# Transformer block on one core: the batch loop written out, maxima computed in head pairs, losses by gram matrices

## What is computed

```
x = layernorm(x + self_attention(x))       # three rounds over the first 16 tokens of a batch; the other rows get its bias alone
q, k, v = heads(x @ Wq), heads(ctx @ Wk), heads(ctx @ Wv)     # 16 heads of 16, ctx has 1601 rows
x = layernorm(x + softmax(q k' / 4 + mask) v @ Wo)
base = x @ W_base + b_base
h[n] = relu(x @ W_enc[n] + b_enc[n])                          # 8 experts, 64 wide
losses[n] = mean((h[n] @ W_dec[n] + b_dec[n] - x) ** 2)       # per batch
a = connected_idx[argmin(losses)]
x = layernorm(x + base + relu(x @ W_down[a] + b_down[a]) @ W_up[a] + b_up[a])
```

## Time and profile before

| | |
|---|---|
| median of 3 runs | 2031.69 us (2022.25 to 2032.2) |
| span of the profiled execution | 2026.6 us |
| own time of the profiled execution | not given beside its span |
| first stage, up to the first score of batch 0 | 0 to 234.0 us |
| batch 0 | 234.0 to 420.0 us |
| a full batch (the fourth) | 857.8 to 1078.1 us |
| last batch | 1735.3 to 1952.8 us |
| tail of the last batch | 1952.8 to 2026.6 us |

### The profile page before, as it was taken

One profiled execution on the slowest core, in us unless ns is written; L12 is line 12 of the kernel. 1 busy time (PEld: TensorE's weight loads), 2 busy tenths in 40 slices (PEclk: granted clock), 3 DMA queues, 4 the chain that ended last, 5 costly groups with the idle time before them and its releaser, 6 DMA issues. The chain is left out here.

```text
span 2026.6 us, 27895 instructions
## 1 busy us (share of the span) xinstructions
PE 1861.2 (92%) x9743; PEld 797.2 (39%) x9743; DVE 1452.2 (72%) x3155; ACT 1122.5 (55%) x2339; POOL 197.4 (10%) x154
## 2 busy tenths in 40 slices
PE   5655899999998999899998999899989999899976
PEld 3441333443344433443344334443344334433442
DVE  3334788777877778687877787777868787778753
ACT  2220177656764667456754676466645675467632
POOL 5511000000000000000010000000001001000000
PEclk7665699999999999999999999999999999899988
DMA  2422435170614233160516061433316051605100
GB/s 95 75 52 40 62 80 84 33 129 23 77 36 85 69 58 54 48 111 25 68 44 130 22 77 36 79 75 57 55 47 114 23 68 44 130 22 77 36 22 13
DMA packets 103957, 125.45 MB, mean 62 GB/s; under 512 B 18595, under 2 KB 88244, under 8 KB 103814
## 3 DMA queue, kind: packets, MB, share of 16 engines
q1 hardware_dynamic: 101282, 122.48, 33.0%
q10 hardware_dynamic: 2532, 1.07, 0.2%
HBM read 84.97 MB, written 38.55 MB: 61 GB/s over the span
## 5 line engine op out<-in xcount | busy, mean ns | idle before, releaser
L1040 DVE TENSOR_REDUCE xneg_max_pieces<-banks 128x1 f32<-128x401 f32 (+1 forms) x2132 | 1116.5, 566 | 206.1 <-PE banks L750 199.0
L883 ACT ACTIVATE xprobs<-banks 128x512 f32<-128x512 f32 x1664 | 865.2, 604 | 600.4 <-PE banks L773 600.4
L750 PE MATMUL banks<-xk_stacks,xq_stacks 97*128 97x401 bf16 (+1 forms) x2132 | 732.7, 345 | 15.4 <-DMA xq_stacks<-parts_dram 13.4
L773 PE MATMUL banks<-xq_stacks,xk_stacks 99*128 99x512 bf16 x1664 | 639.9, 385 | 39.9 <-issue 32.2
L788 PE MATMUL values<-xprobs,xv_rows 128*17 128x512 f32 x3328 | 437.9, 598 | 1.9 <-PEq L1463 1.9
L750 PEld LDWEIGHTS banks<-xk_stacks,xq_stacks 97*128 97x128 bf16 x2132 | 208.4, 98 | 559.5 <-issue 233.7
L773 PEld LDWEIGHTS banks<-xq_stacks,xk_stacks 99*128 99x128 bf16 x1664 | 164.0, 99 | 250.8 <-ACT xprobs L883 85.3
L1097 POOL TENSOR_TENSOR xk_parts<-xk_rest,xk_parts 128x401 bf16<-128x401 f32 (+1 forms) x72 | 66.8, 929 | 951.1 <-ACT xk_parts L844 950.9
L686 PE MATMUL work<-ctxT_sb,xkT 128*128 128x400 f32 (+1 forms) x288 | 116.5, 528 | 13.3 <-DVE xk_rest L991 13.3
L698 PE MATMUL work<-xvT,ctxT_sb 128*128 128x128 f32 (+1 forms) x884 | 119.7, 290 | 5.0 <-DVE xv_rows L1009 5.0
L708 PE MATMUL work<-hT,wdec 128*128 128x512 f32 x240 | 123.5, 595 | 0.8 <-ACT hT L824 0.8
(11 more groups left out here) (188 smaller groups left out, 1081.4 us busy)
## 6 DMA issues: line engine op xcount, KB each, us to landing
xk_stacks<-key_parts_dram SPq DMA_DIRECT2D x102, 400.2 KB
key_parts_dram<-xk_parts SPq DMA_DIRECT2D x162, 100.0 KB, 1.7
ctxT_sb<-in_ctxT SPq DMA_DIRECT2D x9, 1601.0 KB, 14.1
xq_stacks<-parts_dram SPq DMA_DIRECT2D x102, 128.0 KB
parts_dram<-xq_parts SPq DMA_DIRECT2D x54, 128.0 KB, 1.7
key_parts_dram<-xk_parts SPq DMA_DIRECT2D x54, 100.2 KB, 1.7
xa<-in_x SPq DMA_DIRECT2D x9, 512.0 KB, 3.5
x_dram<-xa SPq DMA_DIRECT2D x9, 512.0 KB, 6.6
```

The costliest lines, as they stand in the source:

```text
L750: pe.matmul(mx[n % MRING][:, 0:w], qst[0:R_MAX, k % 2, h, q * P:(q + 1) * P], kst[0:R_MAX, k % 2, h, k0:k0 + w], start=True, stop=True).th ...
L773: pe.matmul(scores[n % SRING], kst[0:ROWS, k, h, t * P:(t + 1) * P], qst[0:ROWS, k, h, :], start=True, stop=True).then_inc(made, 1)
L883: nc.scalar.activation(probs[:, sl % 2, j, :], scores[n % SRING], ACT.Exp).then_inc(exped, 1)
L1040: nc.vector.tensor_reduce(nmp[:, m % 2, x // NP, x % NP:x % NP + 1], mx[n % MRING][:, 0:w], AX.X, ALU.max, negate=True).then_inc(mxr, 1)
```

## The change

- The batch loop, its drains and its clears are gone: all 416 slots are written out in one block, semaphores count on through all batches, and jobs carry their batch (`NOW`, `NEXT`, `PREV`). The last batch prepares nothing.
- Maxima come in pairs of heads, an even and an odd one. The stacks hold the three larger products (`TOP`) and the mask in rows 0 to 48 for even heads and 64 to 112 for odd ones, the three smaller products elsewhere. A pair is two 49-row matmuls in different halves of the array's rows and in two banks, read by one VectorE instruction. So maxima leave out the three smaller products.
- Score banks are two instead of three; pair banks are two times two.
- In a slot the order is: two scores, a pair, the first of two jobs, the values, two scores, a pair, the last job, the third pair. Many jobs stand in other slots; the first key projection for the next batch in slot 5.
- The losses come from `h' G h`, with the gram matrices of the decoder made once in the first stage (`wdT`, `gw`), beside the third round of self-attention: a job `gram` has two float32 matmuls of `wdecT` with x and one of `gram` with h in one bank, four jobs a batch instead of 16 `dec`. VectorE multiplies by h and sums; ScalarE has no squares.
- SyncE's stacks are twice as many transfers, top rows first, by head parity. The context has two buffers and its load is issued behind the stacks of the batch. Key parts have their own DRAM for each half.

```diff
-SRING, MRING = 3, 3
+SRING, MRING = 2, 2
+TOP = 3
+TOP_ROWS = (slice(0, 49), slice(64, 113))
...
+            0: {0: [("v", 0, NOW)], 1: [("otr", 3, PREV)], 2: [("oT", 0, PREV), ("oT", 1, PREV)], 3: [("xo", 0, PREV)],
+                4: [("xo", 1, PREV)], 5: [("kproj", 0, NEXT)], 6: [("v", 1, NOW)], 7: [("kproj", 1, NEXT)],
+                8: [("x1T", 0, NEXT), ("x1T", 1, NEXT)], 9: [("max", 1, NOW)],
...
+            elif name == "gram":
+                for kin in range(CH):
+                    pe.matmul(W[:], wdecT[:, kin, i * P:(i + 1) * P], x2T[:, kin, :], start=kin == 0, stop=False)
+                pe.wait_ge(w_free, ph.order.after(("enc", i, b)))
+                last = pe.matmul(W[:], gram[:, i, :], hT[:, i, :], start=False, stop=True)
...
+            for par in range(2):
+                rows = TOP_ROWS[par]
+                last = pe.matmul(pairs[n % MRING][:, par, 0:w], qst[rows, k, h2, par, q * P:(q + 1) * P],
+                                 kst[rows, k, h2, par, k0:k0 + w], start=True, stop=True)
+            last.then_inc(mxd, 1)
...
+        def pe_slot(m, t):
+            jobs = work_at(m, t)
+            todo = pairs_at(m, t)
+            pe_scores(m, t, 0)
+            pe_scores(m, t, 1)
+            if todo:
+                pe_next_pair(*todo[0])
+            if len(jobs) > 1:
+                pe_job(MAIN, jobs[0])
+            if m or t:
+                pe_values(XKT * m + t - 1)
+            pe_scores(m, t, 2)
+            pe_scores(m, t, 3)
+            if todo:
+                pe_next_pair(*todo[1])
+            if jobs:
+                pe_job(MAIN, jobs[-1])
+            for one in todo[2:]:
+                pe_next_pair(*one)
...
-            nc.vector.tensor_reduce(nmp[:, m % 2, x // NP, x % NP:x % NP + 1], mx[n % MRING][:, 0:w], AX.X, ALU.max,
+            nc.vector.tensor_reduce(nmp[:, of % 2, j2, :, q, piece], pairs[n % MRING][:, :, 0:w], AX.X, ALU.max,
...
+        def sp_stacks(b, c):
+            if b:
+                sp_key_parts_out(2 * (b - 1) + 1 + c)
+                nc.sync.wait_ge(qparts_out, 48 * (2 * (b - 1) + 1 + c))
+            if b or c:
+                before = GROUPS * b - (NG if c == 0 else 0)
+                if before:
+                    nc.sync.wait_ge(made, GH * XKT * before)
+            for top in (True, False):
+                sp_query_stacks(c, top)
+                sp_key_stacks(b, c, top)
...
+        def sp_batch(b):
+            nxt, prev = b + 1, b - 1
+            if nxt < B:
+                sp_load_x(nxt)
+            if prev >= 0:
+                sp_load_x1(prev)
+            sp_stacks(b, 1)
+            if nxt < B:
+                sp_load_ctx(nxt)
+                use = 2 * NP * b
+                if b:
+                    sp_free_key_dram(nxt, 0)
+                sp_key_parts(0, use)
...
-            eng.drain().then_inc(arrived, 1)
-            eng.wait_ge(go, i)
```

More of the change, by code:

```diff
@@ L62, with __init__ @@
 class Phase:
-    def __init__(self, tail, order):
-        self.tail, self.order = tail, Order(order)
+    def __init__(self, first, order, end=()):
+        self.first, self.order, self.end = first, Order(order), frozenset(end)
 class Order:
@@ L725, in normed_of @@
-        def normed_of(ph, what):
-            order = [n for n in ("x1", "x2", "y") if n == "x1" and ph is not LAST or n != "x1" and ph.tail]
-            return order.index(what) + 1
-        def max_event(e):
-            m, x = divmod(e + LEAD * MXS, XKT * MXS)
-            return (m + 1, x) if x < MXG else None
-        MAXES = [max_event(e) for e in range(XSLOTS * MXS)]
-        COUNT = [0]
-        for one in MAXES:
-            COUNT.append(COUNT[-1] + (one is not None))
-        def pe_max_piece(m, x, n):
+            elif name == "wdT":
+                if i == 0:
+                    pe.wait_ge(loaded, N_LOADS)
+                for n in range(NPAIR):
+                    last = pe.transpose(W[:, n * P:(n + 1) * P], wdec[:, n, i * P:(i + 1) * P], ident[:])
+            elif name == "gw":
+                pe.wait_ge(w_free, ph.order.after(("wdT", 1, 0)))
+                for kin in range(CH):
+                    pe.matmul(W[:, 0:P], wdecT[:, kin, i * P:(i + 1) * P], wdecT[:, kin, i * P:(i + 1) * P],
+                              start=kin == 0, stop=kin == CH - 1)
+                for kin in range(CH):
+                    last = pe.matmul(W[:, P:P + 2], wdecT[:, kin, i * P:(i + 1) * P], bdec[:, 2 * i:2 * i + 2, kin],
+                                     start=kin == 0, stop=kin == CH - 1)
@@ new lines, in act_slot @@
+        def act_slot(m, t):
+            sl = XKT * m + t
+            jobs = work_at(m, t)
+            if sl > 1:
+                nc.scalar.wait_ge(summed, sl - 1)
+            act_exp(m, t, 0)
+            act_exp(m, t, 1)
+            if t == 0 and m:
+                act_values_out(m - 1)
+            for one in work_at(*divmod(sl - 1, XKT)) if sl else ():
+                act_later(MAIN, one)
+            if len(jobs) > 1:
+                act_job(MAIN, jobs[0])
+            act_exp(m, t, 2)
+            act_exp(m, t, 3)
+            if jobs:
+                act_job(MAIN, jobs[-1])
+            if m + 1 < B * GROUPS:
+                if t == XKT - LEAD + 1:
+                    act_max_out(MAIN, m + 1)
+                if t == XKT - LEAD + 2:
+                    act_max_in(m + 1, m + 1)
@@ L979, in dve_job @@
             v = nc.vector
[L980 to L981 removed]
+            name, i, b = job
+            if name not in ("kproj", "qproj", "xo", "y", "v", "gram", "loss", "max", "otr", "gw"):
                 return
```

969 lines of the change are left out of this document (485 added, 484 removed).

## The result

The changed kernel takes 2073.7 us (median of 4 runs, 2067.9 to 2075.9) against 2030.8 for the kernel before (4 runs, 2022.3 to 2032.2): a ratio of 1.022, interval 1.019 to 1.024. It is longer, clear of the noise; whether by more than 2% the interval leaves open. The profiled execution took 2074.0 us, 1.9 more than its span of 2072.1, where the forecast had added 5.1. The forecast was 2086, with a span of 2081.

The account below looks back on a forecast made before the run. TensorE sets the pace everywhere but at the iteration's end. Terms -53 - 35 - 24 - 151 + 139 + 63 + 99 + 16 + 6 - 5 = +55 us, span 2081, forecast 2086 us, 2.7% slower; range 1990 to 2120.

Parts of the forecast that it names:

- opening: Before the main part: decoder copies after sixteen exps and gram jobs delay probability transposes 11 us; net +6 us.
- context wait and half speed behind it: Slot 5's first key projection waits for the context behind stack transfers, +99 us; lower clock after it, +16 us.
- all else in the main part: Main-part terms: loop -53, last batch -35, decoder -24, pairs -151, tiling changes +139, two score banks and small waits +63.
- close: After the main part: 17.5 us of decoder become about 12, -5 us.
- Pairs and changes: Main-part maxima: pairs at 0.19 us save 151 us; 2359 tiling changes instead of 896, at 0.095 us, cost 139.
- the main rival: TensorE's row-tiling changes cost nothing, the walk gives 75 us less: 2011 us, -1.0%; chance 0.14.
- the walk: Slot-by-slot reckoning of main-part waits: 69 us for two score banks, 34 for adapter, x1 transpose and small waits.
- Loop, last batch, decoder: Main part: seven iteration ends go, -53 us; last batch prepares nothing, -35; gram jobs replace decoder matmuls, -24.
- hidden ring waits: Rival: 40 of the 69 + 34 us of small waits lie beside other work: 2046 us, +0.7%; chance 0.13.
- quick transfers: Rival: stacks take 20 us, 2021 us, -0.5%; or context in time at no cost, 1971; chance 0.15.
- changes at 0.11 with pairs at 0.2: Upper bound of TensorE's unknown costs, tiling changes 0.11 us and pairs 0.2 us: 2114 us.
- 15 us for a hundredth: TensorE tiling changes: one hundredth of a us on all 2359 is some 15 us of the total.

Follow-up runs that it names:

- the experiment that moves one line: Changed kernel with SyncE issuing the next batch's context first in a batch, before the x, x1 and stack transfers: 2013.5 us, ratio 0.992.
- The pairs on the whole array: Changed kernel with each of a pair's matmuls taking its whole stack's rows (99 and 113 instead of 49), so neither is row-tiled: 2071.3 us, ratio 1.020.
- the third pair's new place: Changed kernel with a slot's third pair moved ahead of the slot's job, right behind the second: 2032.4 us, ratio 1.002.

## Why the prediction was right, and where its terms were off

Its sign and size were right, 2086 against 2074, by mechanisms that the runs confirm in the main. That it came as near as 12 us is partly luck: two of its terms erred by 50 and 37 us in opposite directions.

| part | forecast | measured |
|---|---|---|
| opening | +6 | +10 |
| context wait and half speed behind it | +99 +16 | +65 |
| all else in the main part | -61 | -24 |
| close | -5 | -5 |
| span | +55 | +45 |

The measured column is one trace against one. Openings with the changed kernel's code end at 240.3 to 244.0 us and those of the order before at 234.0 and 237.8, and some 2 us of the close belong to "all else" if both closes are counted alike.

*The context.* Place, cause and count were as told, and the experiment that moves one line takes the waits away. The term was oversized by 50 us. The forecast had the context land 36.6 us after a batch begins, with TensorE there at 23.5. It came at 24.0, but the context was there after 32.1: the stacks went at 131 GB/s, not 123, and SyncE had begun to issue them 0.5 us ahead of the batch's first score. Slot 5 takes 8.7 us more than its 4.43 in the mean of six batches, half speed included, and 12.7 in the first; the prediction had 13.1 + 2.3 and 20.9 + 2.3. The share of this that the end feels is 60 us, by the experiment.

*Pairs and changes.* Both prices held: a pair 0.176 us (forecast 0.19), a change 0.10 at row tiles as at narrow columns (forecast 0.095). The pairs on the whole array and the third pair's new place show it independently, 0.19 us saved against 0.17 paid about a pair, and 0.20 saved in each slot with three pairs. That row changes are free, the main rival, is refuted. One price was left out: a float32 job behind a halved pair pays nearly 0.10 us a second time, between its first two matmuls, 25 us in the main part for which the prediction had nothing. The Trainium skill, TensorEngine Tiling (Array Packing), Tiling Modes, has the rule that a changed mode drains TensorE. The trace agrees for rows and for columns, at 0.10 us; moving between two tiles of one mode cost 3 ns.

*All else in the main part.* This was 37 us too low. I added up TensorE's starts in a full batch (the fourth), each at the lower quartile of the gaps between its two lines, with the values' long gaps left as they are: the engine's own pace is 203 us where it was 208, about 6 less, against 5 forecast. So the engine got faster as reckoned. What is left of a batch without the context's wait (218.9 in the run with the context first) is 16 us of waits, half speed and the jobs' second price; before it was 11 in the mean, of which 8 were the loop's end. So this grew by some 13 us a batch, where the prediction had 8. Two of its steps were mis-sized. It took off 40 us, 5 a batch, for waits of the kernel before, where some 3 a batch stood. And it had nothing for the jobs' second price, some 3 of the 16. Of the rest, 1.5 is half speed behind the x1 transposes in that run, and some 12 are waits, where the walk had 13, though not in the places walked: the x1 transposes wait 2.4 us against 1.7, the adapter, which had 2.7, is waited for by nobody inside a batch, and the exps count for less (some 40 us for 69). Which engine each of the many waits of 0.1 us belongs to I have not resolved.

*Loop, last batch, decoder.* No idle time stands at a batch's border; the last batch takes 189.0 us, 30 less than an unstalled full one, against the 35 forecast for its missing preparation; the decoder of the close takes 12.0 us, as forecast. No run undid these parts alone, so their terms rest on the traces.

*The opening.* The cause was named right: the copies behind the exps, then the gram jobs ahead of the transposes. The trace has 10 us for the forecast's 6, but openings of the same code end up to 4 us apart, so the 6 isn't refuted; moving the copies gave back some 10 us.

*Range and chances.* The range held the time. The 0.13 for hidden ring waits was right in part, since the exps were worth some 40 of 69 us, but the terms beside them took it back; the 0.15 for quick transfers was right in part, 4.5 us a batch. Small slips of its working decide nothing: 27, 7.5 and 2 are 36.5, not 36.6; 982 pairs in 416 slots are 2.36 a slot, not 2.46; changes at 0.11 with pairs at 0.2 give 2118, not 2114; 15 us for a hundredth belong to the 1463 added changes, not to all 2359.

## What to carry to other kernels

Row-packing pays only per group of packed matmuls between two changes of tiling: price the pair with its changes (here 0.17 us saved against 0.19 paid, and 0.29 where a float32 job follows), and then put packed work side by side until the buffer behind it is what waits. A load that frees its own buffer early should be issued ahead of the bulk that fills the queue; the one line that did this was worth 3%. And when one wait goes, look at the next wait behind it: here it did not grow, but the half-clock stretch moved behind it, and a second edit that shortened it made both gains whole. Compare the waits of both traces before a longer slot is called a longer wait.

## What the runs showed of the hardware

- A change between full-array and 49-row matmuls costs 0.093 us going in and 0.100 coming out; from full-array to 17-column matmuls it is 0.092. A float32 job behind the 49-row matmuls starts its second matmul another 0.10 us late (0.213 us after the first, against 0.112 behind full-array pairs). Two matmuls on different halves start 3 ns apart, on the same half 0.18 us.
- VectorE reads a maximum over two banks at once, 2 x 400 elements, in 0.99 us, against 0.57 for one of 401, both with their fixed part.
- A wait of 2.4 us on TensorE at the x1 transposes was followed by a half-clock stretch in all seven batches with the context first, and in one of seven in the changed kernel, where a longer wait and its half-clock stretch came some 16 us sooner; with a wait of 1.3 us at the same place there was none, and the clock stood at 1.00 for whole batches.
- The context transfer, 1.6 MB, landed in 7 us when issued ahead of the stacks and in 18 behind them.
